# Cells stage: the six products of an edge half stand among the short score products of the slot before

## The reference

```python
def _L0_ffn_ref(inputs, ew, act_w, We, be, Wq, Wk, Wv, Wo, ln_g, ln_b):
    NUM_NOD, MAX_PREV, NUM_EDGE, D, H = 6, 5, 20, 256, 8
    nodes = {-1: inputs}
    lind = 0
    for c in range(NUM_NOD):
        nsrc = min(c + 1, MAX_PREV)
        snode = c - nsrc
        eq, ek, ev = (lind + nsrc - 1, lind, lind + nsrc // 2)
        in_q, in_k, in_v = (c - 1, snode, snode + nsrc // 2)
        q = ew[c, 0] * (nodes[in_q] @ We[eq] + be[eq])
        k = ew[c, 1] * (nodes[in_k] @ We[ek] + be[ek])
        v = ew[c, 2] * (nodes[in_v] @ We[ev] + be[ev])
        o = _mha(q, k, v, Wq[c], Wk[c], Wv[c], Wo[c])
        nodes[c] = act_w[c] * o + q
        lind += nsrc
    out = nodes[NUM_NOD - 1]
    return _layernorm(out, ln_g, ln_b)
```

## Time and profile before

| | us |
|---|---|
| median of three runs | 3193.3 (3192.03 to 3195.54) |
| the profiled execution | 3187.25 |
| its span in the profile | 3185.5 |
| PE busy in the span | 3017.8 (95%) |
| PEld busy | 2466.6 (77%) |
| DVE busy | 2186.4 (69%) |
| ACT busy | 2009.2 (63%) |

### The profile page before, as it was taken

How to read it: one execution, slowest core, us unless ns; L and a number is a source line. 1 busy time by engine, 2 the same in 40 slices (tenths; PEclk the granted TensorE clock), 3 DMA queues, 4 the chain that set the end, 5 groups by cost and what they waited for, 6 DMA issues and landing times. The chain is left out here.

```text
span 3185.5 us, 88343 instructions
## 1 busy us (share of the span) xinstructions
PE 3017.8 (95%) x34369; PEld 2466.6 (77%) x34369; DVE 2186.4 (69%) x5188; ACT 2009.2 (63%) x3697; POOL 941.1 (30%) x812
## 2 busy tenths in 40 slices
PE   8999999979999999999979999999999999799999
PEld 7888888857877877877868888788788787564798
DVE  5777777766666666666644788778778877567543
ACT  5777777757767767677743677676666766332444
POOL 3444444337656555555630000000000000111210
PEclk9999999989999999999989999999999999899899
DMA  2111111237888888888885111111111110552000
GB/s 86 47 46 46 46 46 46 57 52 128 151 141 150 151 137 146 152 145 148 156 188 173 35 42 49 55 42 49 56 42 42 54 36 19 179 163 77 7 21 27
DMA packets 643036, 273.37 MB, mean 86 GB/s; under 512 B 549387, under 2 KB 617952, under 8 KB 642736
## 3 DMA queue, kind: packets, MB, share of 16 engines
q1 hardware_dynamic: 613168, 225.13, 33.6%
q10 hardware_dynamic: 29568, 44.05, 4.2%
HBM read 113.37 MB, written 21.50 MB: 42 GB/s over the span
## 5 line engine op out<-in xcount | busy, mean ns | idle before, releaser
L1310 POOL TENSOR_TENSOR front_parts<-wide_prob,front_parts 128x1024 f16<-128x1024 f32 x256 | 549.1, 2146 | 377.5 <-ACT front_parts L1536 318.6
L1629 DVE TENSOR_REDUCE wide_row_max<-wide_score 128x1 f32<-128x1024 f32 x256 | 312.6, 1221 | 167.4 <-PE wide_score L1348 166.5
L1348 PE MATMUL wide_score<-wide_kT,wide_qT 128*128 128x512 f32 x1536 | 414.3, 405 | 4.9 <-ACT wide_prob L1524 3.3
L1524 ACT ACTIVATE wide_prob<-wide_score,wide_neg_max 128x1024 f32<-128x1024 f32 x256 | 285.2, 1114 | 157.3 <-DVE wide_neg_max L1632 151.0
L886 ACT ACTIVATE mask_prob<-mask_prob,mask_row_min 128x256 f32<-128x256 f32 x512 | 232.0, 503 | 161.7 <-DVE mask_row_min L966 161.7
L1348 PEld LDWEIGHTS wide_score<-wide_kT,wide_qT 128*128 128x128 f32 x1536 | 277.5, 190 | 66.0 <-issue 8.9
L1536 ACT ACTIVATE front_parts<-wide_prob 128x1024 f16<-128x1024 f32 x256 | 269.8, 1054 | 16.8 <-ACT wide_prob L1524 8.3
L2472 DVE TENSOR_REDUCE cell_row_max<-cell_score 128x8 f32<-128x512 f32 x192 | 131.0, 682 | 148.5 <-PE cell_score L2097 146.6
L117 POOL TENSOR_TENSOR cell_var_eps<-cell_mean_var,const_eps 128x4 f32<-128x4 f32 x8 | 1.6, 202 | 651.9 <-DVE cell_mean_var L111 651.9
L1364 PE MATMUL wide_turn<-front_probT,wide_v 128*128 128x256 f16 x1536 | 189.5, 273 | 2.5 <-DMA front_probT<-front_parts 2.5
L1364 PE MATMUL wide_pv<-front_probT,wide_v 128*128 128x256 f16 x1536 | 189.9, 273 | 0.5 <-DMA front_probT<-front_parts 0.5
(11 more groups left out here) (364 smaller groups left out, 6845.6 us busy)
## 6 DMA issues: line engine op xcount, KB each, us to landing
cell_w_stage<-cell_weights ACTq DMA_DIRECT2D x24, 768.0 KB, 6.1
mask_ctx<-in_ctx SPq DMA_DIRECT2D x32, 512.0 KB, 3.9
ctx_ctx<-in_ctx SPq DMA_DIRECT2D x32, 512.0 KB, 4.2
mask_mask<-in_mask_BxS_ik SPq DMA_DIRECT2D x32, 256.0 KB, 4.0
front_probT<-front_parts SPq DMA_TRANSPOSE x512, 3.2
cell_w_stage<-in_L_ffn_We ACTq DMA_DIRECT2D x24, 256.0 KB, 2.7
cell_w_stage<-in_L_ffn_Wo ACTq DMA_DIRECT2D x24, 256.0 KB, 3.1
front_x_all<-in_x SPq DMA_DIRECT2D x32, 128.0 KB, 2.0
```

Source lines behind the costliest of these rows:

```text
L1310: pool.tensor_tensor(parts[:, s % 2, LO, :], prob[:, s % 2, :], parts[:, s % 2, HI, :], ALU.subtract).then_inc(part_lo, 1)
L1348: mm = pe.matmul(score[:, s % 2, half * 512:(half + 1) * 512], qT[:, u_par, a, s * P:(s + 1) * P], kT[:, par, b, half * 512:(half + 1) * 5 ...
L1524: act.activation(prob[:, s % 2, :], score[:, s % 2, :], ACT.Exp, bias=neg_max[:, s % 2:s % 2 + 1], scale=SHARP, accum_out=row_sum[:, u_par ...
L1629: dve.tensor_reduce(row_max[:, one], score[:, s % 2, :], AX.X, ALU.max).then_inc(max_found, 1)
```

## The change

The first edge half of slot n + 1 no longer stands at the head of slot n + 1. Its six products are put into `scores` of slot n, for the same attention order: product 0 ahead of the first half of the scores, 1 in the middle of that half, 2 between the halves, 3 in the middle of the second half, 4 and 5 behind the scores. The waits that stood before it (`acc_copied`, and `set_lo` for X = 0) are taken by `edge_ready`, ahead of `scores`. For the first slot of all, and in the last round's last cell, the six stand in one row as before. The second half (`close_edge`) stays where it was. The number of matmuls is the same, and the other engines' lists keep their order.

```diff
-        def scores(use, proj):
+        def scores(use, proj, edge_of=None):
+            def edge_part(n):
+                if edge_of is not None:
+                    edge_product(edge_of, 0, n)
 
             pe.wait_ge(proj_copied, proj)
+            edge_part(0)
             for hf in range(DH):
 
                 pe.wait_ge(ring_copied, use + hf + 1)
                 for s in range(SUB):
+                    if s == 2:
+                        edge_part(1 + 2 * hf)
                     for b in range(2):
...
                             if s == SUB - 1 and b == 1 and hf == DH - 1:
                                 mm.then_inc(score_ready, 1)
+                edge_part(2 + 2 * hf)
+            edge_part(5)
...
-        def add_edge(oh, a, c, X, set_no, use):
...
+        def edge_product(source_node, oh, n):
+            j, ih = n // DH, n % DH
+            a_, b_ = PASSES[j]
+            pe.matmul(acc[oh][:, :], weight(a_, EDGE_AT, ih, half(oh)), source_node[:, b_, ih, :], start=(n == 0), stop=False)
+
+        def edge_ready(a, c, X, set_no):
+            if not isinstance(a, int) or a >= 1:
+                pe.wait_ge(acc_copied, a * DH)
+            if X == 0:
+                pe.wait_ge(set_lo, set_no * 2 + 1)
+            return node[:, X, :, place(source[c][0])]
+
+        def edge_behind(i, c, X):
+            c_next, X_next = (c, 1) if X == 0 else ((c + 1) % NODES, 0)
+            return edge_ready(attention(i, c, X) + 1, c_next, X_next, set_number(i, c) + X)
+
+        def close_edge(c, X, use):
+            for n in range(6):
+                if n == 5:
+                    pe.wait_ge(ring_copied, use + LATE_AT + ROW - EARLY)
+                edge_product(node[:, X, :, place(source[c][0])], 1, n)
...
-                add_edge(0, a, c, X, set_no, use)
                 turn_late(use, a, X)
-                add_edge(1, a, c, X, set_no, use)
+                close_edge(c, X, use)
...
-                    scores(use + Q_AT, proj_at(i, c, X) + PROJ_SLOT)
+                    scores(use + Q_AT, proj_at(i, c, X) + PROJ_SLOT, edge_behind(i, c, X))
...
-                    scores(use + Q_AT + DH, proj_at(i, c, X) + PROJ_LAST)
+                    scores(use + Q_AT + DH, proj_at(i, c, X) + PROJ_LAST, edge_behind(i, c, X))
```

More of the change, by code:

```diff
@@ L2185, in _ @@
         turn_early(2 * DH, 0, 0)
+        first_source = edge_ready(0, 0, 0, 1)
+        for n in range(6):
+            edge_product(first_source, 0, n)
         def body(i, last):
@@ L2203, in body @@
                     turn_output(use + output_at(X, final), 0)
+                    if X == 0:
+                        behind_source = edge_behind(i, c, X)
+                        for n in range(6):
+                            edge_product(behind_source, 0, n)
                 elif c < NODES - 1:
```

## The result

| us | before | changed |
|---|---|---|
| median | 3194.4 (4 runs) | 3233.1 (3229.3 to 3236.4, 4 runs) |
| profiled execution | 3187.25 | 3233.0 |
| its span | 3185.5 | 3231.3 |

The changed kernel takes 1.0118 times as long, 95% interval 1.0101 to 1.0136: 38.7 us more by the medians. Forecast: 34 more, 3227 within 3203 to 3243.

What follows compares the result with a forecast made beforehand. TensorE's own list was taken to bound the cells stage. Direct cost 23 us, plus 13 for DVE's lateness, less 2 of stalls, gave +34 us on 3193.3, so 3227 us, 1.1% slower, range 3203 to 3243.

Steps and rivals of the forecast that it cites:

- Bound: Cells stage: TensorE's own instruction list bounds it, PE busy 185.2 of 189 us in round 0, so added time counts almost whole.
- Place: From the start of the last q product to the first transpose of `turn_late`: 3.51 us before, 4.06 after, 0.55 more.
- Direct sum: Over the 46 changed places: 25 at 0.55 us more and 21 at 0.45 more, 23 us in all.
- gave back (2): Of the 2.9 us of stalls without a releaser inside the scores, 2 us were expected to go away.
- DVE's lateness: DVE starts 0.92 us later against `turn_late`, so PE waits longer for `oT`: 13 us in all, bounds 0 and 42.
- 0.38 of slack: X = 0 slots, c1 to c4: slack before the output products absorbs 0.38 of 0.92 us, leaving 0.55 of new wait.
- the four that I counted as immune: Of 16 X = 0 slots, c1 to c4, four add no wait, as something else already gave PE over a microsecond.
- c5 X0: Slots where PE already waits 1.48 us for the low part of `oT`: all 0.92 us comes on top.
- Rival 1: Changes of tile shape (drains) are paid, but DVE absorbs its lateness: 3214 us, chance 0.14.
- rival 3: In `scores`, a lone product hides the short weight loads, so each place costs 0.5 us less: 3170 us, chance 0.08.
- rival 4: The change moves nothing, through slack elsewhere, or stalls without a releaser going away and drains costing half: 3193 us, chance 0.07.
- rival 2: Score runs of 32 go at the slower mean pace, or DVE's lateness reaches further slots: 14 us more, 3241, chance 0.11.

Runs made afterwards that it cites:

- filler_full: The kernel before, plus three extra full-array matmuls a place, where the changed kernel has lone products: 3244.6 us, ratio 1.0168 to the kernel before.
- the fillers: Two runs, the kernel before plus three extra matmuls a place: full-array ones, 3244.6 us; ones of the scores' own tile shape, 3231.3 us.
- the break counts: Runs reordering the changed kernel's edge products: product 1 alone between score halves, 3202.9 us; products 1 to 3 in one row there, 3215.5 us.
- after_pool: The changed kernel with the low part of the fused weights computed on GpSimd instead of DVE: 3202.2 us, ratio 1.0028 to the kernel before.
- before_pool: The kernel before with only the low part of the fused weights moved from DVE to GpSimd: 3183.9 us, ratio 0.9968 to the kernel before.
- four_ahead: The changed kernel with edge products 0 to 3 in one row ahead of unbroken scores, 4 and 5 behind: 3200.1 us, ratio 1.0017 to before.
- one_ahead: The changed kernel with edge product 0 ahead of unbroken scores and 1 to 5 behind: 3181.5 us, ratio 0.9956 to the kernel before.

## Why the prediction was right

*Bound.* TensorE's list: shown. filler_full adds 57.2 us to the places of its trace and 51.6 us to the median.

*Place.* 4.06 forecast, 4.07 measured. That it is the change of tile shape which costs, is shown by the fillers, by the break counts and by the transposes above. The distances 0.14, 0.34 and 0.32 in the earlier trace rows were enough to price it.

The rule on draining of "TensorEngine Tiling (Array Packing)", Key Properties, of the Trainium skill agrees with these rows. The pull-ahead of loads of "TensorE: Matmul & The Clock Gate", Part 2, of the Trainium skill did not cover a change of shape here: the first short load starts with its matmul (2311.94, 2311.95), where the first load of the transposes starts 0.23 ahead of its own (2285.65, 2285.88).

```profile
2311.94 0.35 PEld L2105 LDWEIGHTS cell_score<-cell_kT,cell_qT 32*64 32x64 f32 x32 [0.35 <-issue]
```

*Direct sum.* 23 forecast. The places sum to 17.2 more, but before they held more stalls without a releaser: 9.9 against 4.5 us by the waits. Without these the places grew by 22.6. The stalls inside the scores went from 2.9 to 0.2, as I gave back (2), and the one at the back edge from 5.2 to 4.3.

*DVE's lateness.* The mechanism was right, the term too small: 13 forecast, 25.0 measured. DVE starts 1.01 late against `turn_late` for 0.92 forecast.

The first step that was mis-sized is the 0.38 of slack that I took off in the c1 to c4 X = 0 slots. At the start of the output products it held: they come 0.69 later, so some 0.3 of the lateness was absorbed (`project_k`, which waits for the fused weights, comes 0.28 later; that lies inside the 0.69). But DVE's chain goes on behind that step, and I stopped there. The first output product now stands behind a wait and takes 0.34 to the next where it took 0.23, and each of the two rows of `turn_early` waits for DVE's division:

```profile
2322.81 0.73 PE L2174 MATMUL cell_acc<-cell_oT,cell_w 128*128 128x512 f32 x2 [0.28 <-DVE cell_oT L2444]
2323.15 0.39 PE L2174 MATMUL cell_acc<-cell_oT,cell_w 128*128 128x512 f32 x1
```

```profile
PEld cell_ring L2118 <- DVE cell_prob L2515: 6.3, 30, 0.2
```

That wait was 2.9 us in 14 times before. The output products take 2.93 to `turn_early` (2322.81 to 2325.74) where they took 2.79, and `turn_early` 0.94 (2325.74 to 2326.68) where it took 0.79. So 0.29 is added to the 0.69, and nearly all of the 1.01 passes through: the rest of such a slot went from a median of 15.72 to 16.69 us, 0.97 more where my term was 0.55. It did in 13 of the 16 slots. The other three, c4 X0 in rounds 1 to 3, had held 0.7 to 0.9 us more than the others before, and grew by 0.03 to 0.26 only: so the four that I counted as immune were three.

The second is the count of the slots that have no slack. The term has five c0 X0 and c5 X0 slots; the 46 have seven, which grew by 9.2 us where I had 4.6. after_pool and before_pool together show that the 25 us are DVE's: with its 1.75 us moved away, 2.1 of them are left.

*c5 X0.* 0.92 forecast a slot, 2.0 measured: 0.99 in the first, 2.5 and 2.6 in the other two. There the clock comes in, below; it is some 3 of the 25.0 us.

*Rivals.* Rival 1 (DVE absorbs its lateness) is refuted by four_ahead and after_pool, rival 3 (faster) by the 0.43 behind each lone product, rival 4 by the result. Of rival 2 the first half (slower runs of 32) is refuted by the 0.27 in each run; the second half, that DVE's lateness costs more than I had, came true, with 12 us for its 14, though more by costing more in the same slots than by reaching further ones.

*Luck.* That the total came within 5 us is partly luck. The lateness was 12 us short, and 3.4 us of that were offset, as 5.4 us of stalls without a releaser went and not 2. Moreover the two profiled executions moved by 45.7 us, 12 over the forecast, where the medians moved by 38.7; of the 45.7, 4.5 lie ahead of the first slot (1751.49 and 1755.99), where nothing was changed.

## What to carry to other kernels

Count changes of tile shape in TensorE's list as instructions of their own: read the start-to-start distance across one in the trace, and put work of one shape in one row. Filling a wait with products of another shape paid here only at the ends of the short run; of the orders tried, one product ahead won the most without the move to GpSimd. And when work is put ahead of what releases another engine, follow that engine's chain to every step that waits for it, not to the nearest one with slack.

## What the hardware showed beyond that

The wait of PE in c5 X0 could cost clock as well. Windows of the changed kernel (us, busy by engine, granted clock), the wait and the products behind it:

```profile
2222.00:2224.60 2.60, 0.15 (x2) 0.00 (x0) 2.56 (x5) 1.64 (x4) 0.00 (x0) 1.00 0.00 0
2224.60:2228.70 4.10, 4.07 (x13) 3.14 (x14) 4.03 (x8) 1.65 (x3) 0.00 (x0) 0.69 0.00 0
```

```profile
2224.64 4.25 PE L2174 MATMUL cell_acc<-cell_oT,cell_w 128*128 128x512 f32 x12 [2.48 <-DVE cell_oT L2444]
```

The second fence is the timeline of PE with these products. After 2.48 us of idle the granted clock averages 0.69 over the products, so part of them ran at 1.2 GHz in place of 2.4; twelve take 4.25 us. Before, the wait in this slot was 1.48 and the window behind it had the full clock:

```profile
2199.00:2203.00 4.00, 4.00 (x20) 2.93 (x20) 3.93 (x8) 2.52 (x5) 0.00 (x0) 1.00 0.00 0
```

It happened in two of the three c5 X0 slots among the 46; each of the two took 1.5 us more than the first, which had the same wait of 2.48 us and a full clock behind it (1.00 from 1967 to 1973). So a wait of DVE's making can be charged more than its length. The length alone does not decide it: in one_ahead two waits of 1.7 us were followed by half the clock for most of the products, the third was not:

```profile
2205.10:2209.00 3.90, 3.83 (x10) 3.01 (x11) 3.83 (x8) 0.99 (x3) 0.00 (x0) 0.56 0.00 0
```

Those two slots of one_ahead took 1.5 us more than its third as well. What decides which of the waits is charged was not tried. And GpSimd's subtraction of 128 x 1536 at 3.5 us beside DVE's work brought no loss that the medians show.
